# Transformer block on one core: both parts of the key-bias weight in one 32-column product, and two more VectorE operations

## The reference

```
q = (layernorm(x) @ Wq + bq) -> 16 heads of 64
k = (ctx @ Wk + bk)          -> 16 heads of 64
scores = q . k / 8;  attn = softmax(scores);  out = attn . v
```

## Time and profile before

| | |
|---|---|
| median of three runs (lowest to highest) | 2145.27 us (2142.52 to 2146.36) |
| span of the profiled execution, the only time it has | 2145.9 us |
| PE busy / PE weight load busy | 2097.1 / 1850.5 us |
| DVE / ACT / POOL busy | 1568.1 / 1271.4 / 946.7 us |
| cross attention, about 28 to 1370 us: PE busy | 1334.2 of 1342 us |
| key-bias products in the span | 192, in 16 places |
| VectorE operations on their result (L719) | 64, in 16 places |

### The profile page before, as it was taken

One profiled execution on the slowest core, in us unless ns is written; L12 is line 12 of the kernel. 1 busy time (PEld: TensorE's weight loads), 2 busy tenths in 40 slices (PEclk: granted clock), 3 DMA queues, 4 the chain that ended last, 5 costly groups with the idle time before them and its releaser, 6 DMA issues.

```text
span 2145.9 us, 46808 instructions
## 1 busy us (share of the span) xinstructions
PE 2097.1 (98%) x15864; PEld 1850.5 (86%) x15865; DVE 1568.1 (73%) x2774; ACT 1271.4 (59%) x3067; POOL 946.7 (44%) x800
## 2 busy tenths in 40 slices
PE   8999999999999999999999999899998999999997
PEld 7898899899899888888898998678886888888886
DVE  7667767767767677677677676699996877666665
ACT  5566666656656665666656666377774335555553
POOL 5323322322333332233223223288884234777775
PEclk9999999999999999999999999999999999999999
DMA  5000000010010010000100100255533222333332
GB/s 156 11 21 25 24 20 24 10 34 20 15 34 20 15 34 15 20 24 10 34 24 10 34 10 1 63 160 158 166 117 101 87 73 56 55 54 53 54 54 42
DMA packets 100687, 103.91 MB, mean 48 GB/s; under 512 B 11953, under 2 KB 90161, under 8 KB 100625
## 3 DMA queue, kind: packets, MB, share of 16 engines
q1 hardware_dynamic: 86992, 84.47, 12.6%
q0 software_dynamic: 13632, 18.62, 5.4%
HBM read 72.52 MB, written 30.54 MB: 48 GB/s over the span
## 4 chain that ended last, share of the span: by engine, by line
PE 76%; POOL 10%; issue 6%; DVE 4%; ACT 2%; DMA 2%; POOLq 0%; DVEq 0%; ACTq 0%
PE banks L933 38%; PE banks L976 6%; PE banks L1006 5%; PE banks L1021 5%; PE banks L1034 5%; POOL out_dram L2434 4%; PE banks L1675 3%; POOL r_x L2398 3%; PE banks L2273 2%; POOL index L2405 2%; DMA out_dram<-r_y,index 2%; PE banks L1738 1%; PE banks L963 1%; PE banks L1697 1%; PE banks L1754 1%
## 5 line engine op out<-in xcount | busy, mean ns | idle before, releaser
L933 PE MATMUL banks<-ctxT_hi,qk_hi 128*128 128x256 f32 x1024 | 300.2, 293 | 0.0
L933 PE MATMUL banks<-ctxT_hi,qk_lo 128*128 128x256 f32 x1024 | 289.1, 282 | 0.0
L933 PE MATMUL banks<-ctxT_lo,qk_hi 128*128 128x256 f32 x1024 | 286.8, 280 | 0.0
L567 ACT ACTIVATE probs<-banks,nbias 128x256 f32<-128x256 f32 x512 | 236.9, 488 | 77.7 <-DVE nbias L700 77.3
L453 POOL TENSOR_TENSOR rinv<-rsum,inverse 128x4 f32<-128x4 f32 x96 | 96.8, 1008 | 396.8 <-ACT probs L567 396.8
L574 ACT ACTIVATE pc<-banks 128x512 f32<-128x512 f32 x256 | 153.3, 599 | 190.9 <-PE banks L933 187.8
L658 DVE TENSOR_TENSOR qk_lo<-banks,qk_hi 128x512 fp32r<-128x512 f32 x256 | 163.6, 685 | 87.9 <-ACT qk_hi L529 87.8
L695 DVE TENSOR_REDUCE peak<-banks 128x4 f32<-128x1024 f32 x128 | 156.3, 1221 | 80.0 <-PE banks L933 80.0
L933 PE MATMUL banks<-pT_hi,ctx_hi 128*128 128x512 f32 x512 | 205.1, 401 | 1.7 <-DVE pT_lo L658 1.7
L658 DVE TENSOR_TENSOR pT_lo<-banks,pT_hi 128x512 fp32r<-128x512 f32 x256 | 164.4, 683 | 57.1 <-ACT pT_hi L529 56.6
L933 PE MATMUL banks<-pT_hi,ctx_lo 128*128 128x512 f32 x512 | 202.2, 395 | 0.0
(11 more groups left out here) (271 smaller groups left out, 6165.7 us busy)
## 6 DMA issues: line engine op xcount, KB each, us to landing
ctx_raw<-in_ctx_dram SPq DMA_DIRECT2D x64, 256.0 KB, 2.7
experts_w<-in_L_ffn_We_dram SPq DMA_DIRECT2D x24, 512.0 KB, 4.0
x_in<-in_x_dram SPq DMA_DIRECT2D x16, 256.0 KB, 2.8
x_again<-in_x_dram SPq DMA_DIRECT2D x16, 256.0 KB, 2.8
x_stream<-z SPq DMA_DIRECT2D x16, 256.0 KB, 2.1
s_x<-x_stream SPq DMA_DIRECT2D x32, 128.0 KB, 3.8
s_x_again<-x_stream SPq DMA_DIRECT2D x32, 128.0 KB, 3.2
x_normalised<-s_xl SPq DMA_DIRECT2D x32, 128.0 KB, 1.7
```

The source lines that it names most:

```text
L567: nc.scalar.activation(probs[:, s % 2, p, :], scores[:, s % 2, p // 2, (p % 2) * SK:(p % 2 + 1) * SK], ACT.Exp, bias=nbias[:, s % 2, p:p + ...
L933: last = nc.tensor.matmul(out, a, b, start=(n == 0), stop=(n == 3 * len(pairs) - 1))
```

## The change

The two parts of the weight are stored side by side, `wqb_both`, so that one product with 32 moving columns gives `xT_hi` by upper in columns 0 to 15 and `xT_hi` by lower in columns 16 to 31. The product of `xT_lo` with the upper part is added to the first 16 columns. A tile has four products in place of six, a `qbk` eight in place of twelve. VectorE copies the first halves from PSUM to a new buffer `xb`, adds the second halves, and the four operations that write `qbk` read `xb`. Copy and add are both linked, so the next operation waits for each. The bank is still freed by the last of the four.

```diff
-LINKS_PER_GROUP = 33
+LINKS_PER_GROUP = 35
...
-    wqb_hi = sb("wqb_hi", [P, DC, HEADS], F32R)
-    wqb_lo = sb("wqb_lo", [P, DC, HEADS], F32R)
+    wqb_both = sb("wqb_both", [P, DC, 2, HEADS], F32R)
+    wqb_hi, wqb_lo = wqb_both[:, :, 0, :], wqb_both[:, :, 1, :]
+    xb = sb("xb", [P, TILES, HEADS])
...
             bank, free = wait_filled(dve, g, key)
+            halves = bank[:, 0:TILES * 2 * HEADS].rearrange("p (n w h) -> p n w h", n=TILES, w=2)
+            link(nc.vector.tensor_copy(xb[:, :, :], halves[:, :, 0, :]))
+            link(nc.vector.tensor_tensor(xb[:, :, :], xb[:, :, :], halves[:, :, 1, :], ALU.add))
...
-                        in0=bank[rows, 0:TILES * HEADS].rearrange("p (n m e) -> p n m e", n=TILES, e=2)[:, :, :, hp],
+                        in0=xb[rows, :, :].rearrange("p n (m e) -> p n m e", e=2)[:, :, :, hp],
...
-                last = exact3(bank[:, n * HEADS:(n + 1) * HEADS],
-                              [((xT_hi[:, c, at], xT_lo[:, c, at]), (wqb_hi[:, c, :], wqb_lo[:, c, :]))
-                               for c in range(DC)])
+                both = bank[:, n * 2 * HEADS:(n + 1) * 2 * HEADS]
+                for c in range(DC):
+                    nc.tensor.matmul(both, xT_hi[:, c, at], wqb_both[:, c], start=(c == 0), stop=False)
+                for c in range(DC):
+                    last = nc.tensor.matmul(both[:, 0:HEADS], xT_lo[:, c, at], wqb_hi[:, c, :],
+                                            start=False, stop=(c == DC - 1))
```

More of the change, by code:

```diff
@@ L482, in gpsimd @@
                         weights_by_bk(half, c)
-                nc.gpsimd.tensor_copy(wqb_hi[:, :, :], wqb[:, 0:DC, :]).then_inc(wqb_step, 1)
+                nc.gpsimd.tensor_copy(wqb_hi, wqb[:, 0:DC, :]).then_inc(wqb_step, 1)
                 pool.wait_ge(wqb_step, WQB_STEPS * DC * 2 + 1)
-                nc.gpsimd.tensor_tensor(wqb_lo[:, :, :], wqb[:, 0:DC, :], wqb_hi[:, :, :],
+                nc.gpsimd.tensor_tensor(wqb_lo, wqb[:, 0:DC, :], wqb_hi,
                                         ALU.subtract).then_inc(wqb_done, 1)
```

## The result

| | before | after |
|---|---|---|
| median of the runs taken together (lowest to highest) | 2144.81 us (2142.52 to 2146.36) | 2155.35 us (2151.06 to 2156.37) |
| span of the profiled execution | 2145.9 us | 2152.9 us |

The change makes the kernel slower: the ratio is 1.0043, 95% interval 1.0030 to 1.0055, thus 9 us. That is the other side of the forecast and outside its range. The profiled spans lie 7.0 us apart, the medians 10.5: wherever a profiled execution has both, its time is 1.7 to 1.8 above its span, so by an estimate the execution profiled before took 2147.6 us, more than any of the four runs in the table.

The account below looks back on a forecast made before the run. TensorE's queue was taken to set the time. 15 places in step 7 x 0.02 = +0.3 us, the start 0, gave 2146.2 against the profiled 2145.9; less 0.6, a median of 2145.6 us, range 2141.5 to 2150 (8 in 10).

Parts of the forecast that it names:

- Products: TensorE in step 7: products of 32 columns stay 0.112 us apart, so four fewer save 0.45 us at each place.
- Copy and add: VectorE ahead of the four qbk operations: two new linked operations, 0.19 us each plus 0.035 for each link.
- E: Time that copy and add put on VectorE ahead of the last qbk operation: 0.45 us, bounds 0.39 to 0.56.
- the rival of short operations: The four qbk operations, reading SBUF instead of PSUM, take half of their 0.18 us each: 2140.2 us, chance 6%.
- The wait: TensorE at pt 1 in step 7 waits 0.62 us for bank 1, seen free 0.05 after VectorE's end.
- its own sign of being wrong: In step 7: the wait absent or under 0.3 us, or the turn over 0.3 us longer.
- From that load to the first score's load it is 0.39 us.: TensorE behind the wait for bank 1: pt 1's first load to the first score's takes 0.39 us, read in step 3.
- 0.02: Net change per group in step 7: the first score's load comes 0.02 us later, in general E - 0.43.
- 0.28 to spare: Kernel before, pt 1 in step 7: bank 1 seen free at 779.28, wanted at 779.56, so 0.28 us of slack.
- The third rival: Loop's turn laid bare: register operation and branch run only after the wait, 0.39 us a turn, 2151.4 us, chance 8%.
- The start: The 16th place, qbk0: peak stays at 31.44, effect put at 0, bounds -0.45 and +1 us.
- the fourth rival: VectorE's four operations with two SBUF inputs stand behind GpSimd, up to 1.27 us a turn: 2164.7 us, chance 3%.

Follow-up runs that it names:

- the last two timed kernels: Changed kernel with bank 1 freed by the add, qbk0 from PSUM and jump moved: 0.9965; kernel before with only the jump moved ahead of pt 0: 0.9990.

## Why the prediction was wrong

- **Products.** Right: eight products, 0.112 apart, and four are worth 0.45 (turns of 83.40 and 83.85, the last two timed kernels).
- **Copy and add.** Right: 0.18 and 0.19 us, VectorE's last operation 0.72 + 0.44 behind the copy's start, E = 0.45. From SBUF the four kept their 0.72 in the loop, so the rival of short operations fell.
- **The wait.** Right in place and size: 0.58 for `pt` 1, where 0.62 was worked out, and load at VectorE's end + 0.05. The turn is 0.35 us longer, which is past the 0.3 that the prediction set as its own sign of being wrong.
- **"From that load to the first score's load it is 0.39 us."** This step failed. It was read from step 3, where no jump lies between. It is 0.78 here, and 0.39 once the jump is moved: the jump's steps and those for the scores run behind the wait and take 0.77. The score's load came 0.85 behind VectorE's end before and comes 0.84 behind it now (means of the 13 turns with a jump), so nearly all of the 0.44 by which VectorE's work is longer goes into the turn, and not 0.02. Measured are 0.36 a turn; the other 0.07 are won earlier in the turn, where TensorE reaches the folds of step 7 0.07 sooner, and that isn't traced further.
- **"0.28 to spare."** Also wrong, for the same reason: before, bank 1 is seen free at 779.28 and the score's load is at 780.10, 0.82 later. The floor was reached already; the slack that looked like 0.28 was none, and what VectorE's chain gains in length goes into the turn. There was a sign: from `pt` 1's load to the score's it was 0.54 without a wait and 0.39 with one. TensorE's own pace is 0.44, as the two ends without a jump in the same trace show (0.44 at 108 and at 1282 us); the 0.54 held 0.10 of the jump.
- **The third rival** named this mechanism, its 0.39 us and its sum, 2151.4 us, and got 8%. The ground against it, that four transposes cover the jump, took for granted that what the sequencer does is shorter than their 0.39. No row gave its length. It runs beside them, as the doubled transposes show, but it takes 0.77, of which 0.47 is the jump. That the sum, 2151.4, lies closest of all to the measured time is part luck, since it has no term for the start.
- **The start.** Put at 0, with +1 at most; it was 2.7. Of it 1.2 has come in by the time `pT_hi` of the first step is written on ScalarE (39.23 instead of 38.05), behind the four operations held by GpSimd (the peak is at 32.97 instead of 31.44). Making `qbk0` from PSUM gave back only 0.5 of it, and other operations with two SBUF inputs took long there. That is the fourth rival, where GpSimd does work at that time: it was priced for the loop and not for the one place where the earlier trace rows shows GpSimd busy. The other 1.5 lie beside the lower clock: 24 scores took 4.38 us, and 2.89 before. The chains of waits, before and then changed:

```profile
51.03 2.89 PE banks L933 x24
...
52.20 4.38 PE banks L937 x24
```

  The held operations don't bring that clock about: three kernels of the change with a `qbk0` that isn't held had it too.

## What to carry over

Where a loop turns, look at the last wait of the engine that sets the time: what the loop's jump costs is hidden only if it can run well before that engine's work runs dry. If the last wait comes late, rotate the loop so that the jump lies ahead of it, or free the buffer from a copy rather than from the last reader. A price for "from the wait to the next work" must be read at a place with the same instructions between, the ones that don't count as busy included; and a small edit has to be priced at its first, uneven run as well as in the steady loop.

## What was unexpected of the hardware

- Where the last wait is late, the first weight load of a turn comes 0.77 to 0.83 us after TensorE's sequencer has passed it, in nine kernels, whether four or eight transposes lie between; without the jump it is 0.39 to 0.52. The sequencer stands at a wait while the engine still has loads to do, so a late wait can cost though no idle time stands before it.
- A compare-and-branch of TensorE that jumps back took 0.21 to 0.24 us, and the next step started 0.27 after its start (785.36 to 785.62); the one that leaves the loop took 0.08. The Trainium skill, "Advanced Engine Details and Errata", section "Control Flow Timing", gives a compare-and-branch about 108 ns, which is neither of the two.
- A semaphore raised by VectorE's sequencer behind a linked add let the next operation start 0.36 after the add's start and 0.17 after its end; in the kernel where the add's own end frees the bank, the next operation follows the add's start by 0.22 (778.19 to 778.41).
- Four copies of 64x16, SBUF to SBUF, can take 2.63 us beside GpSimd's casts and subtractions, where four operations with an input from PSUM took 0.73.
